# A graph network's last attention layer: fp32 sums as three fp32r passes, and the heads before it in another order

## The reference, cut to what matters

```
h = (x @ W).reshape(n, heads, out_c)
e = leaky_relu((h . a_src)[src] + (h . a_dst)[dst], 0.2)
ex = exp(e - segment_max(e, dst)[dst])
alpha = ex / (segment_sum(ex, dst)[dst] + 1e-16)
out = segment_sum(h[src] * alpha, dst) + bias
...
h = elu(gat_layer(x, W1, ..., heads=8, out_c=96, concat=True))
out = gat_layer(h, W2, ..., heads=1, out_c=768, concat=False)
x = layernorm(x + out)
```

## Time and profile before

| | |
|---|---|
| median of three runs | 1436.75 us (1436.01 to 1437.41) |
| the profiled execution | 1437.73 us, span of its instructions 1436.0 us |
| busy TensorE, VectorE, ScalarE, GpSimd | 1367.7, 762.8, 441.9, 559.0 us |
| mean granted TensorE clock | 0.991 of full speed |
| the eight heads of `Q2` | about 1249 to 1352 us of the span |
| `Q3` | about 1352 us to the end |

### The profile page before, as it was taken

The page is one execution under the profiler, slowest core; times in us unless marked ns, Lnnn a source line. Parts: engine busy times, 40 slices in busy tenths (PEclk is TensorE's granted clock), DMA queues, the critical chain, the costliest instruction groups (busy, mean ns, idle before and its releaser), DMA issues.

```text
span 1436.0 us, 22503 instructions
## 1 busy us (share of the span) xinstructions
PE 1367.7 (95%) x7784; PEld 1274.6 (89%) x7784; DVE 762.8 (53%) x1818; ACT 441.9 (31%) x936; POOL 559.0 (39%) x629
## 2 busy tenths in 40 slices
PE   5999999999999999999999999999998999988997
PEld 3676999999999999999999999999888887878874
DVE  6876755224544356474232434765375504599644
ACT  1564521102010000100110222255574424467631
POOL 8000324324243525343442423143433463548830
PEclk9999999999999999999999999999999999998999
DMA  3101111113333223242211211221101310200001
GB/s 117 55 29 34 39 34 50 50 34 109 105 107 105 67 89 115 72 131 68 67 55 45 68 53 46 61 83 57 56 23 39 107 53 17 82 18 1 1 11 54
DMA packets 57804, 86.49 MB, mean 60 GB/s; under 512 B 6468, under 2 KB 54459, under 8 KB 57584
## 3 DMA queue, kind: packets, MB, share of 16 engines
q1 hardware_dynamic: 45204, 65.82, 15.8%
q10 hardware_dynamic: 12504, 19.36, 4.4%
HBM read 83.24 MB, written 1.92 MB: 59 GB/s over the span
## 4 chain that ended last, share of the span: by engine, by line
PE 76%; DVE 13%; ACT 4%; issue 3%; POOL 3%; DMA 1%; DVEq 0%; SPq 0%; ACTq 0%; POOLq 0%
PE psum L2487 13%; PE psum L2491 13%; PE psum L2490 13%; PE psum L2504 7%; PE psum L2507 7%; PE psum L2988 4%; DVE max_scratch L2189 3%; PE psum L2636 3%; PE psum L2561 2%; POOL w_lo L919 2%; PE psum L2530 1%; PE psum L2533 1%; PE psum L2476 1%; DVE more_tiles L2233 1%; DVE score_tiles L2233 1%
## 5 line engine op out<-in xcount | busy, mean ns | idle before, releaser
L2487 PE MATMUL psum<-w_lo,xT_hi 128*125 128x384 f32 (+4 forms) x1110 | 377.4, 340 | 3.3 <-POOL w_lo L919 1.8
L2491 PE MATMUL psum<-w_hi,xT_hi 128*125 128x384 f32 (+4 forms) x1110 | 373.4, 336 | 0.0
L2490 PE MATMUL psum<-w_hi,xT_lo 128*125 128x384 f32 (+4 forms) x1110 | 373.3, 336 | 0.0
L906 POOL CAST w_hi<-w_raw 128x384 fp32r<-128x384 f32 x190 | 105.2, 553 | 569.7 <-PE psum L2491 466.0
L1093 ACT ACTIVATE h_hi<-psum 125x384 fp32r<-125x384 f32 (+1 forms) x120 | 59.1, 492 | 529.3 <-PE psum L2491 524.9
L1739 DVE TENSOR_TENSOR h_lo<-psum,h_hi 125x384 fp32r<-125x384 f32 (+1 forms) x120 | 66.9, 558 | 288.0 <-ACT h_hi L1093 287.2
L2487 PEld LDWEIGHTS psum<-w_lo,xT_hi 128*125 128x125 f32 (+1 forms) x1110 | 205.9, 186 | 6.1 <-POOL w_lo L919 3.4
L908 POOL TENSOR_TENSOR w_lo<-w_raw,w_hi 128x384 fp32r<-128x384 f32 x190 | 201.2, 1059 | 15.2
L2490 PEld LDWEIGHTS psum<-w_hi,xT_lo 128*125 128x125 f32 (+1 forms) x1110 | 206.4, 186 | 0.4
L2491 PEld LDWEIGHTS psum<-w_hi,xT_hi 128*125 128x125 f32 (+1 forms) x1110 | 206.0, 186 | 0.0
L2504 PE MATMUL psum<-h_lo,adjacency 125*125 125x384 f32 (+3 forms) x600 | 203.5, 339 | 2.1 <-issue 1.9
(11 more groups left out here) (350 smaller groups left out, 2272.2 us busy)
## 6 DMA issues: line engine op xcount, KB each, us to landing
w_raw<-weights_dram SPq DMA_DIRECT2D x296, 192.0 KB, 2.4
score_w_raw<-weights_dram ACTq DMA_DIRECT2D x58, 192.0 KB, 2.8
x_nat<-x_dram SPq DMA_DIRECT2D x1, 1875.0 KB
x_residual<-x_dram SPq DMA_DIRECT2D x5, 375.0 KB
score_a_rows<-L_gnn_a_src_dram ACTq DMA_DIRECT2D x8, 192.0 KB, 3.3
score_a_rows<-L_gnn_a_dst_dram ACTq DMA_DIRECT2D x8, 192.0 KB, 4.5
out_dram<-x_residual SPq DMA_DIRECT2D x4, 375.0 KB
rgcn_bias<-rgcn_bias_dram SPq DMA_DIRECT2D x1, 1125.0 KB
```

The costliest lines, as they stand in the source:

```text
L906: nc.gpsimd.tensor_copy(mem.wh[:, slot, :], mem.raw[:, raw_slot, :]).then_inc(w_hi_ready, 1)
L2487: ins = nc.tensor.matmul(o, h, wl, start=(j == 0), stop=False, skip_group_check=True)
L2490: nc.tensor.matmul(o, l, wh, start=False, stop=False, skip_group_check=True)
L2491: ins = nc.tensor.matmul(o, h, wh, start=False, stop=stop and j == k - 1, skip_group_check=True)
```

## The change

In the last layer the features and the probabilities are each split into an fp32r high part (ScalarE: `last_hi`, `prob_hi`) and a low part (VectorE: `last_lo`, `prob_lo`), and each fp32 product of the sums becomes three fp32r ones: high by low, high by high, low by high (`last_part`). The unit of 385 columns is widened to 386. Blocks 0 and 1 are summed together as the tiles come (`last_first_block`, and one tile behind it `last_second_block`), the other three after them. The output banks are 5, 6, 2, 3 instead of 0 to 3. Two scores now stand ahead of the first finish.

The last bias is loaded at the start of `Q2` and added to the residual by GpSimd ahead of the heads' products, not in `Q3`.

In the heads, VectorE makes the columns ahead of the third score (`COLUMNS_AT`) and a head's two finishes right behind its own third score (`FINISH_AT`), not behind z. ScalarE finishes the exponential of the third tile before it takes the fourth. GpSimd's order becomes: first product, sum of the head before, second and third product, bias.

`Q1` sends at place 22 instead of 16 (`LONG_EVENTS`).

```diff
@@ -157,15 +157,16 @@
     def out_bank(self, u):
...
-        return u % self.out_banks
+        return (5, 6, 2, 3)[u % 4] if self.index == 3 else u % self.out_banks
...
 PAIR_EVENTS = {3: (("scores", 0),), 6: (("row", 0),), 16: (("send", 0),)}
+LONG_EVENTS = {3: (("scores", 0),), 6: (("row", 0),), 22: (("send", 0),)}
...
                {0: ((1, 0), (4, 1)), 1: ((7, 2), (10, 3))})
-Q1 = Attention(Q0, 1, D, K8, PIECES, True, BASE_L2B, True, PAIR_EVENTS, {})
+Q1 = Attention(Q0, 1, D, K8, PIECES, True, BASE_L2B, True, LONG_EVENTS, {})
...
@@ -703,7 +713,7 @@
         LAST = HEADS3 - 1
-        LATE = 3
+        LATE, COLUMNS_AT, FINISH_AT = 3, 2, 2
...
@@ -1002,10 +1012,15 @@
-
-            def late_products(h):
-
-                for i, counts in enumerate(late_counts):
+            pool.wait_ge(last_bias_loaded, 16)
+            pool.wait_ge(xT_lo_ready, T_Q[2] + UNITS)
+            for m in range(NB):
+                r = mem.xres[0:BP, m, :]
+                nc.gpsimd.tensor_tensor(r, r, mem.par[0][0:BP, 0:D], ALU.add).then_inc(res_biased, 1)
+
+            def late_products(h, a, e):
+
+                for i, counts in list(enumerate(late_counts))[a:e]:
...
@@ -1025,20 +1040,15 @@
                 nc.gpsimd.tensor_tensor(t, t, e, ALU.add).then_inc(layer_ready, 1)
...
-            late_products(0)
+            late_products(0, 0, LATE)
             for h in range(LAST):
-                late_products(h + 1)
-                unit_bias(h)
+                late_products(h + 1, 0, 1)
...
                     unit_sum(h - 1)
+                late_products(h + 1, 1, LATE)
+                unit_bias(h)
...
-
-            pool.wait_ge(params_loaded, 16 * 9)
-            pool.wait_ge(cols_ready, Q3.head0 + 1)
-            for m in range(NB):
-                r = mem.xres[0:BP, m, :]
-                nc.gpsimd.tensor_tensor(r, r, mem.par[1][0:BP, 0:D], ALU.add).then_inc(res_biased, 1)
...
@@ -1384,6 +1394,42 @@
                             keep_row(h)
...
+            def last_hi(g):
+
+                piece, m = g // NB, g % NB
+                act.wait_ge(gemm_done, Q3.gemm0 + g + 1)
+                nc.scalar.activation(mem.last_hi[0:BP, m, piece * HW:piece * HW + HW], bank(Q3.banks[g], 0, HW), ACT.Copy
+                                     ).then_inc(feat_hi_ready, 1)
+
+            def prob_hi(k):
+
+                act.wait_ge(tile_ready, made_by_vector(Q3, 0, k))
+                nc.scalar.activation(mem.prob_hi[k][0:BP, :], source_tile(Q3, 0, k), ACT.Copy).then_inc(prob_hi_ready, 1)
+
+            def last_features():
+
+                for m in range(NB):
+                    if m == NB - 1:
+                        split_hi(Q3.chunk + WRING)
+                    act.wait_ge(gemm_done, Q3.gemm0 + m + 1)
+                    ins = nc.scalar.activation(mem.al[0:BP, m, 0:2], bank(Q3.banks[m], HW, HW + 2), ACT.Copy)
+                    if m == NB - 1:
+                        ins.then_inc(al_ready, 1)
+                    last_hi(m)
+                act.wait_ge(al_turned, Q3.index + 1)
+                a = row_col(Q3)
+                nc.scalar.activation(mem.al_T[0:2, 0:4 * BP], ps[0:2, a:a + 4 * BP], ACT.Copy)
+                nc.scalar.activation(mem.al_T[0:2, 4 * BP:N], ps[0:2, a + 512:a + 512 + BP], ACT.Copy).then_inc(al_copied, 1)
+                split_hi(NCHUNKS)
+                keep_flat(Q3, 0)
+                source_exp(Q3, 0, 0)
+                source_exp(Q3, 0, 1)
+                for k in range(NB):
+                    prob_hi(k)
+                    last_hi(NB + k)
+                    if k + 2 < NB:
+                        source_exp(Q3, 0, k + 2)
...
@@ -1497,6 +1543,7 @@
             load_row("L3_gnn_b1", par[1], D)
+            load_part("L3_gnn_b2", par[0], 0, D, last_bias_loaded)
...
@@ -1531,7 +1578,9 @@
                 source_below(h, NB - LATE)
-                for k in range(NB - LATE, NB):
+                source_exp_below(h, NB - LATE)
+                source_below(h, NB - LATE + 1)
+                for k in range(NB - LATE + 1, NB):
...
@@ -1552,8 +1601,7 @@
                 turn_hi_x3(n)
-            load_row("L3_gnn_b2", par[1], D)
-            feature_product(Q3)
+            last_features()
...
@@ -2153,18 +2201,43 @@
             ins.then_inc(counts_kept, 1)
...
+            def last_lo(g):
+
+                piece, m = g // NB, g % NB
+                dve.wait_ge(feat_hi_ready, g + 1)
+                part = slice(piece * HW, piece * HW + HW)
+                nc.vector.tensor_tensor(mem.last_lo[0:BP, m, part], bank(Q3.banks[g], 0, HW),
+                                        mem.last_hi[0:BP, m, part].bitcast(F32), ALU.subtract).then_inc(gemm_read, 1)
+
+            def prob_lo(k):
+
+                dve.wait_ge(prob_hi_ready, k + 1)
+                nc.vector.tensor_tensor(mem.prob_lo[0:BP, 1 + k, :], source_tile(Q3, 0, k), mem.prob_hi[k][0:BP, :].bitcast(F32),
+                                        ALU.subtract).then_inc(prob_lo_ready, 1)
...
             def scores_begin(q):
...
-                v = mem.feat[0:BP, 0:NB * q.heads * q.w].rearrange("p (h w) -> p h w", w=q.w)
-                link(nc.vector.memset(v[:, :, q.c:q.w], 1.0))
+                if q is Q3:
+                    one = mem.ones[0:BP, 0:2 * NB].rearrange("p (m c) -> p m c", m=NB)
+                    nc.vector.tensor_copy(mem.last_hi[0:BP, :, D:D + 1], one[:, :, 0:1])
+                    nc.vector.tensor_tensor(mem.last_hi[0:BP, :, D + 1:D + 2], one[:, :, 0:1], one[:, :, 1:2], ALU.subtract)
+                    nc.vector.tensor_tensor(mem.last_lo[0:BP, :, D:D + 2], one, one, ALU.subtract)
+                else:
+                    v = mem.feat[0:BP, 0:NB * q.heads * q.w].rearrange("p (h w) -> p h w", w=q.w)
+                    link(nc.vector.memset(v[:, :, q.c:q.w], 1.0))
...
                                         ALU.add)
+                if q is Q3:
+                    for m in range(NB - 1):
+                        last_lo(m)
...
                 nc.vector.tensor_tensor(lo_, mem.al[0:BP, :, 0:q.heads], hi_.bitcast(F32), ALU.subtract).then_inc(al_split, 1)
+                if q is Q3:
+                    last_lo(NB - 1)
...
@@ -2403,9 +2476,12 @@
                 for k in range(NB):
-                    if k == NB - 1 and h + 2 < HEADS3:
+                    if k == COLUMNS_AT and h + 2 < HEADS3:
...
                     score(Q2, h, k)
+                    if k == FINISH_AT:
+                        for i in range(NB - LATE):
+                            finish(Q2, h, i)
...
@@ -2414,8 +2490,6 @@
                     head_z(h - 1)
-                for k in range(NB - LATE):
-                    finish(Q2, h, k)
...
@@ -2440,11 +2514,16 @@
             scores_of(Q3, 0)
+            score(Q3, 0, 0)
+            score(Q3, 0, 1)
+            finish(Q3, 0, 0)
             for k in range(NB):
-                score(Q3, 0, k)
-                if k:
-                    finish(Q3, 0, k - 1)
-            finish(Q3, 0, NB - 1)
+                if k + 2 < NB:
+                    score(Q3, 0, k + 2)
+                if k + 1 < NB:
+                    finish(Q3, 0, k + 1)
+                prob_lo(k)
+                last_lo(NB + k)
...
@@ -3002,20 +3081,7 @@
                         pe.wait_ge(feat_biased, NB * (q.index + 1))
-                if q.index == 3 and j == 0:
-                    for k in range(NB):
...
-                elif q.heads == 1:
+                if q.heads == 1:
...
@@ -3205,8 +3271,40 @@
             chunks_and_scores(Q3, mem.xh, mem.xl)
-            for j in range(NB):
-                sum_tile(Q3, j)
+            def last_part(b, u, k):
+
+                a, width = Q3.units[u]
+                width += width % 2
+                o, p_hi, p_lo = bank(Q3.out_bank(u), 0, width), mem.prob_hi[k][0:BP, nodes(b)], mem.prob_lo[0:BP, 1 + k, nodes(b)]
+                f_hi, f_lo = mem.last_hi[0:BP, k, a:a + width], mem.last_lo[0:BP, k, a:a + width]
+                ins = nc.tensor.matmul(o, p_hi, f_lo, start=(k == 0), stop=False, skip_group_check=True)
+                if owed[0]:
+                    ins.then_inc(w_used, 1)
+                    owed[0] = False
+                nc.tensor.matmul(o, p_hi, f_hi, start=False, stop=False, skip_group_check=True)
+                ins = nc.tensor.matmul(o, p_lo, f_hi, start=False, stop=(k == NB - 1), skip_group_check=True)
+                if k == NB - 1:
+                    ins.then_inc(part_done, 1)
+
+            def last_first_block(k):
+
+                pe.wait_ge(prob_lo_ready, k + 1)
+                pe.wait_ge(gemm_read, Q3.gemm0 + NB + max(k + 1, 2))
+                last_part(0, 0, k)
+                last_part(0, 1, k)
+
+            def last_second_block(k):
+
+                if k == 0:
+                    pe.wait_ge(tile_scored, scored(Q3, 0, NB - 1))
+                last_part(1, 2, k)
+                last_part(1, 3, k)
+
+            in_steps((last_first_block, 0), (last_second_block, 1))
+            for u in range(4, 2 * NB):
```

(3 more changed lines are left out.)

20 lines of the change are left out of this document (9 added, 11 removed).

## The result

The changed kernel took 1451.43 us (median of four runs, 1450.43 to 1453.06), the kernel before 1436.67 on the same chip: a ratio of 1.0104 with a 95% interval of 1.0086 to 1.0121. Slower was right; the 14.8 us are two and a half times the forecast's 5.9, and the time lies 3.4 us above the stated range of 1430 to 1448. The profiled execution took 1450.99, its span is 1449.3.

A forecast was written before the change was run, and what follows sets the result against it. It took TensorE's fp32 sums to bound the last layer's end and VectorE the heads. Send +1.6, heads +13.8 and last layer -9.5 gave +5.9 us: 1442.7 median, likeliest 1439.6 to 1445.5, range 1430 to 1448.

The forecast's parts named there:

- The last layer: Last layer's sums: 150 fp32r products replace 50 fp32 ones and start after 1.8 us without half clock; gain 9.5 us.
- The heads: Third layer's eight heads: the new orders make VectorE's column steps and finishes wait for GpSimd; together +13.8 us.
- the upper bound of +17.5: Heads: the loss if each linked column step waits behind one GpSimd instruction, three waits; +17.5 us.
- the next slips in at the start of the following product: Column step in a whole head: its second instruction passes as GpSimd's next product begins; waiting instead makes the sum 3.5 us worse.
- the three whole heads: Heads with maxima beside GpSimd's full row: 1.5 us more than 11.38 each, +4.5 us for three.
- the heads without maxima: Two late heads: 11.5 us against 8.86, with one finish behind a product; +2.6 us each, +5.2 together.
- The last head's late products: Last head: GpSimd's third product comes behind the sum instead of ahead; +1.4 us.
- The front of head 0: Ahead of the first head: column step into the bias adds, +2.3 us, and finishes ahead of the last score, +1.4.
- The head from 1 to 2: The stretch between these heads, where GpSimd has no sum yet: -1.0 us.
- rival 3: Heads: every linked step waits, and TensorE starts the last GEMM at half clock; 1446 to 1448 us; chance 0.15.
- The send: Second layer: sending at place 22 comes 1.55 us later and delays the slow parameter load, which ends last; +1.6 us.
- The extra load: Last bias's load: one issue on ScalarE's queue, hidden by its wait for the next product; uncovered about 0.3 us.

The follow-up runs named there:

- e1: Kernel before with only the last layer's three split passes; heads' order, bias place and send as before: 1432.79 us, ratio 0.9966.
- e3: Changed kernel, but the last bias loaded and added behind the heads, as before: 1452.92 us, ratio 1.0103.
- e8: e1 with the last bias loaded early and added by GpSimd right behind its last sum of the heads: 1427.43 us, ratio 0.9936.
- e10: e8 with VectorE's and ScalarE's order of the heads from the change, GpSimd's as before: 1433.55 us, ratio 0.9977.
- e12: e8 with both orders of the heads from the change, VectorE's with ScalarE's and GpSimd's: 1445.80 us, ratio 1.0059.
- e15: e8 with the second layer's send at product 22 as in the change: 1430.37 us, ratio 0.9953.
- e14: Changed kernel, but GpSimd's three products of a head multiply by the constant one instead of a second operand: 1444.38 us, ratio 1.0041.
- e9: Changed kernel, but the third layer's column steps read one SBUF operand instead of two: 1451.76 us, ratio 1.0100.
- e13: Changed kernel, but the third layer's column steps are reductions over an axis of one element, from one SBUF operand: 1446.95 us, ratio 1.0070.

## Why the prediction was right or wrong

**The last layer** was right, in mechanism and size: -9.4 us from its columns on, and -8.7 with the 0.7 that its first GEMM loses at half clock, for -9.5. The low parts cost 0.81 and 0.55 for the 0.8 and 0.6 assumed, and the clock stayed at 1.00 behind the 1.46 us of standing still. It rested on the additions being gone from there, and that alone is worth 5.3 us (e1, e3 against e8), of which the prediction saw only the finishes' 1.67.

**The heads** were mis-sized: +21.0 us up to the last layer's columns, 20.3 of them up to the last z, for +13.8. That is above even the upper bound of +17.5 (which the text's own terms make 17.1: 1.1 more for each of three heads). The step that failed first is "the next slips in at the start of the following product". It doesn't: the second instruction is ready 0.10 us after the third product has begun (1317.98 and 1317.88) and waits for its end. The row that the step leaned on shows no slipping in. In the trace of before the finish came 0.01 us after the product and took no longer than alone, and it was the product that waited: the two products of the earlier trace rows took 3.75 us together, where one that meets nothing takes 1.29 in the changed kernel.

```profile
1303.62 0.77 DVE L2241 SCALAR_TENSOR_TENSOR more_tiles<-more_tiles,counts_all 125x625 f32<-125x625 f32 x1
```

So the three whole heads lose 2.1 each and not 1.5, 6.4 us for 4.5. In the heads without maxima both finishes wait, not one: +3.6 and +3.0 for +2.6 each. The last head's late products cost 3.7 for 1.4; the sum had no term for TensorE's half clock behind the wait for them, which makes 2.2 of it. The front of head 0 cost 4.7 for 3.7. The head from 1 to 2 gained the 1.0 forecast. So this was rival 3's mechanism, given 0.15, and its 1446 to 1448 was too low as well. The Trainium skill's rule on two SBUF operands ("SBUF — State Buffer", Who interferes with whom), which the prediction quotes against itself, has each of these steps wait, and the trace agrees (0.60, 1.43 and 1.13 us); the walk went past it.

What none of the cases named is that the larger part of the loss, 11.1 of 19.6 us, needs both orders (e10 to e12). With GpSimd's old order its two-operand work lies beside instructions that read PSUM, and its one-operand minimum beside the column step. The sum ahead of the products turns that round.

**The send** was +1.6, and its mechanism held. This pair of traces shows 0.4, e15 against e8 1.56, and all traces together 1.2 (ten with the late send 64.97 on average, seven without 63.80). In all 17 traces the second layer's first z comes 27.1 us (27.05 to 27.20) after GpSimd takes up the loaded parameters, so the load is what ends last. The late send moves its issue from 25.6 to 25.8 us behind the columns to 26.9 to 27.1, 1.3 later for the 1.55 forecast. The load itself took 10.5 to 11.7 us up to GpSimd's start, with either send; in this pair it was 11.38 before and 10.43 after, which hides most of the price. That e15 comes so near to 1.6 is in part the luck of two loads. TensorE waits for nothing at the send and longer behind it (4.3 us), as the prediction says.

The send's second price was in no term of the sum: with the late send the third layer's columns came after 26.3 to 26.4 us in nine of ten traces (25.3 in e14, whose clock was 0.90 from 1220 to 1230 instead), without it after 24.8 in all seven. That it comes with the send is shown; why the clock falls there is open. In the nine it falls 99.0 us after its fall behind the send. The busy shares of 1220 to 1230 hardly differ (8.62 of 10 us after, 8.64 before), and TensorE's two longest times of standing still in the 10 us ahead of the third layer's columns are the same with either send (0.85 and 1.29 us in e8, 0.86 and 1.29 in e15).

**The extra load** cost nothing, as forecast (e3; e8, which has it too, reaches the third layer's columns in 24.83 as before).

Sum of spans: -0.3 at the start, +0.4 second layer, +1.6 third layer's clock, +20.3 heads, +0.7 clock in the last layer's first GEMM, -9.4 last layer: +13.3, from 1436.0 to 1449.3. Against the forecast's +5.9 that is 6.5 more in the heads, 2.3 for the two falls of the clock that had no term, 0.1 less gain in the last layer, and 1.5 less in the second layer and the start.

## What to carry to other kernels

Before the order of one engine is changed, lay its row beside the other's and mark which instructions read PSUM, which one SBUF operand and which two. Here GpSimd's two-operand work cost nothing beside VectorE's reads of PSUM (0.81 for a maximum with or without it), while a chain of linked small VectorE instructions beside it paid up to one whole GpSimd instruction for each link (0.60, 1.43 and 1.13 us). Test a bundle's parts on a clean base, in pairs too: here one part gained 9.2 us, and the two orders lost more than twice as much together as apart.

## What the runs showed of the hardware that was not expected

A VectorE instruction of five elements waits as long with one SBUF operand as with two in the scalar form (1.43 us in e9 and 1.43 in the changed kernel), and not as a reduction (0.16, e13). A GpSimd product with one operand held VectorE's two-operand instructions up for its first 0.57 us of 1.78 only (e14): a step that came 0.17 us after its beginning took 0.56, steps that came 0.70 or more after it 0.16 to 0.17. Six more blocks, 18 products, ahead of a send were followed by a second fall of the clock in the next layer's GEMM, 99 us after the first, in nine of ten traces.
